# Second expert choice: threshold search by digits and ranks by products, in place of 32 rounds of the eight largest

## The chip, the cores and the metric

The kernel runs on one core of one Trainium2 chip. The metric is the device time of one execution in microseconds (us); before the change it was 1473.17 us, the median of three runs (1472.64 to 1475.16). Work is spread over TensorE (PE in the rows, PEld for its weight loads), VectorE (DVE), ScalarE (ACT), GpSimd (POOL) and the queues of SyncE (SP).

## The reference

Two layers on x of 4 x 1024 tokens of 256 numbers, each a cross attention and a mixture of experts. The change concerns the second mixture, where each expert chooses its tokens. It is this:

```python
k = S // E * CAPACITY            # 1024 // 8 * 2 = 256 tokens for each batch and expert
affinity = softmax(einsum('bsd,ed->bse', x, gate_w), axis=-1)
gating, idx = top_k(transpose(affinity, (0, 2, 1)), k)
x_in = x[bidx, idx]
h = silu(einsum('bekd,eid->beki', x_in, w_gate)) * einsum('bekd,eid->beki', x_in, w_up)
x_e = einsum('beki,edi->bekd', h, w_down)
out = zeros_like(x).at[bidx, idx].add(gating[..., None] * x_e)
```

So there are 32 lists (4 batches x 8 experts) of 256 tokens out of 1024. The order within a list doesn't matter, since the results are added to their tokens; ties at the threshold must go to the lower token number. In front of it stands the second attention: 32 tiles of 128 tokens, 16 heads, 77 keys, then a residual, a second normalisation and the eight gate logits of each token.

## The kernel before

Everything in fp32 precision is done with three products of f16 halves (`mm3`). Each engine has its own program; they meet in semaphores, and each stage's steps are put in an order by hand (`PE_ORDER` and its fellows), run as a software pipeline by `pipeline`: the first and last steps are unrolled, the middle ones run in a loop, unless `straight` asks for all of it unrolled. A `Chain` makes each instruction of a serial computation wait for the one before it.

The second attention (`attn1_*`) runs over 32 tiles t. TensorE makes the transposes, the scores (psS1), the turned probabilities and the outputs; VectorE makes statistics, the row maxima (`largest`, L1571, from psS1 into mx1, then `maxima`, L1580, which scales mx1 in place), the low halves and the residual; ScalarE makes the exponentials and the high halves; GpSimd normalises the probabilities (L1406, L1411). SyncE stores the residual to out_x and the normalised rows to n_rows, 1024 bytes a row. At its end VectorE makes the softmax over the experts: the affinities `aff` (L1616).

The expert choice (`topk_*`) follows. TensorE turns the affinities into 64 rows (each list in two halves) of 512 columns, psA (L1723). VectorE copies them (L1736), and then, 32 times, takes the eight largest of each row (L1739), their places (L1740) and blanks them (L1741), so that each half list has its 256 largest in order. Two such lists are merged: one is turned against the other, and of each pair the larger is one of the 256 largest of the whole (L1742 to L1758). The results are gval (gates) and gidx (token numbers), both with the list in the columns. In this time ScalarE and GpSimd prepare the first expert's weights: ScalarE scales them and makes the high halves (L1706, L1708), GpSimd subtracts these to make the low halves (L1718), two pieces of 3072 columns. SyncE has their loads under way from the last tile of the attention on.

The second expert stage (`ffn1_*`) runs over 16 blocks j of 512 tokens, two for each expert. GpSimd gathers four times 128 rows by gidx (L1785) and at the end adds the results to out_x by the same indices (L1794). TensorE transposes the rows, makes the two up products (psG, psU) for eight pieces f of 128 hidden numbers, then the down product of the block before. ScalarE makes the silu (L1867) and scales the results by gval (L1878); VectorE makes the hidden rows (L1908), their f16 copy (L1911) and their low half (L1913). Both also prepare the next expert's weights piece by piece (L1852, L1891), and the high and low halves of the gathered rows (L1861, L1899).

Of the kernel before, what the change touches and what calls it, by code (L numbers as in the profile page):

```python
# [22 lines left out]
F32 = mybir.dt.float32  # L23
# [122 lines left out]
def program(nc, a, out, tab, n0_rows, x1_rows, n_rows):  # L146
    ctx = ExitStack()
    with ctx:
# [13 lines left out]
        aff = sb("aff", [P, S // P // 2, 2, B, E])  # L162
        gval = sb("gval", [P, 2 * S // E // P, B * E])
# [156 lines left out]
        afff = aff[:].rearrange("p t h b e -> p (t h b e)")  # L320
# [1036 lines left out]
        c_tick = sem("c_tick")  # L1357
# [14 lines left out]
        def apart(e, sem_, value):  # L1372

            wait(e, sem_, value)
            if not isinstance(value, int):
                e.sem_inc(c_tick, 1)

        def attn1_sync(sp):
            def store(t, par):
                sp.wait_ge(c_xn[1], t + 1)  # L1380
                sp.dma_start(out_rows[bass.ds(t * P, P), :], X[:, bass.ds(t, 1), :].rearrange("p t d -> p (t d)"))\
                  .then_inc(c_out[par], 16)
                sp.dma_start(n_rows[bass.ds(t * P, P), :], xn1[1][:, bass.ds(par, 1), :].rearrange("p n d -> p (n d)"))\
                  .then_inc(c_out[par], 16)
            pipeline(sp, T, 1, [(0, store)])
# [34 lines left out]
        def attn1_scalar(act):  # L1420
# [35 lines left out]
            in_order(act, steps, ACT_ORDER, T)  # L1456
# [3 lines left out]
        def attn1_tensor(pe):  # L1460
# [65 lines left out]
            in_order(pe, steps, PE_ORDER, T)  # L1526

        def attn1_vector(dve):
            def stats(n):
                def run(t, par):  # L1530
                    row = X[:, bass.ds(t, 1), :].rearrange("p t d -> p (t d)")
                    if n == 1:
                        apart(dve, c_res, t + 1)
                    dve.bn_stats(st1[n][:], row).then_inc(c_mv[n], 1)
                return run

            def moments(n):
                def run(t, par):
                    apart(dve, c_mv[n], 2 * t + 1)
# [36 lines left out]
            def maxima(half):  # L1576
                def run(t, par):
                    m = mx1[:, half * HP:(half + 1) * HP]
                    dve.wait_ge(c_mx[half], t + 1)
                    dve.tensor_scalar(m, m, -1.0 / (SX * SM), None, ALU.mult).then_inc(c_sub[half], 1)  # L1580
# [20 lines left out]
            in_order(dve, steps, DVE_ORDER, T)  # L1601
# [11 lines left out]
            HT = S // P // 2  # L1613
            for b in range(B):
                tiles = slice(b * 2 * HT, (b + 1) * 2 * HT)
                dve.tensor_tensor(aff[:, :, :, b, :], lex[:, tiles, :].rearrange("p (h t) e -> p t h e", h=2),  # L1616
                                  lsum[:, tiles].rearrange("p (h t) -> p t h", h=2).unsqueeze(3).to_broadcast([P, HT, 2, E]),
# [18 lines left out]
        gx = sb("gx", [P, 2, NT, D], F32, f1)  # L1636
# [8 lines left out]
        HB = 2 * B * E  # L1645
        at_ = sb("at_", [HB, S // 2], F32, f1)
        tv = sb("tv", [HB, CAP], F32, f1)
        ti = sb("ti", [HB, CAP], U32, f1)
        tif = sb("tif", [HB, CAP], F32, f1)
        tvr = sb("tvr", [HB, CAP], F32, f1)  # L1650
        tir = sb("tir", [HB, CAP], F32, f1)
        boff = sb("boff", [P, B * E], F32, f1)
        better = sb("better", [P, SLT, B * E], F32, f1)
        tok = sb("tok", [P, SLT, B * E], F32, f1)
        diff = sb("diff", [P, SLT, B * E], F32, f1)
        f1.close()
        pk = ExitStack()
        psA = ps("psA", [HB, S // 2], F32, pk)
        psV = ps("psV", [P, 4, SLT, HB], F32, pk)
# [18 lines left out]
        d_hid = sem("d_hid")  # L1678
        d_hl = sem("d_hl")
# [6 lines left out]
        k_dve = sem("k_dve")  # L1686
        k_off = sem("k_off")
        k_pe = sem("k_pe")
        ROUNDS = CAP // 8
        KSTEPS = 10 + 3 * ROUNDS  # L1690

# [11 lines left out]

# [6 lines left out]
        def topk_gpsimd(pool):  # L1710
            pool.wait_ge(c_aff, 8)
            pool.iota(boff[:], [[S, B], [0, E]], base=0, channel_multiplier=0,
                      allow_small_or_imprecise_dtypes=True).then_inc(k_off, 1)
# [6 lines left out]
        def topk_tensor(pe):  # L1720
            pe.wait_ge(c_aff, 8)
            for t in range(S // P // 2):
                last = pe.transpose(psA[:, t * P:(t + 1) * P], aff[:, t, :, :, :].rearrange("p h b e -> p (h b e)"), ident[:])  # L1723
            last.then_inc(k_pe, 1)
            pe.wait_ge(k_dve, 3 + 3 * ROUNDS)
            for m, lists in enumerate((tv, tif, tvr, tir)):
                for n in range(SLT):
                    last = pe.transpose(psV[:, m, n, :], lists[:, n * P:(n + 1) * P], ident[0:HB, 0:HB])
            last.then_inc(k_pe, 1)

        def topk_vector(dve):


            ch = Chain(dve, k_dve, 0, KSTEPS)
            dve.wait_ge(k_pe, 1)
            ch(dve.tensor_copy(at_[:], psA[:]))  # L1736
            for r in range(ROUNDS):
                cols = slice(8 * r, 8 * r + 8)
                ch(dve.max(tv[:, cols], at_[:]))  # L1739
                ch(dve.max_index(ti[:, cols], tv[:, cols], at_[:]))  # L1740
                ch(dve.match_replace(at_[:], tv[:, cols], at_[:], -1.0))  # L1741
            ch(dve.tensor_copy(tif[:], ti[:]))  # L1742
            dve.tensor_copy(tvr[:], tv[:, ::-1])
            ch(dve.tensor_copy(tir[:], tif[:, ::-1]))


            first, second = slice(0, B * E), slice(B * E, HB)
            dve.wait_ge(k_pe, 2)
            dve.wait_ge(k_off, 1)
            ch(dve.tensor_copy(gval[:], psV[:, 0, :, first]))  # L1750
            ch(dve.tensor_tensor(better[:], gval[:], psV[:, 2, :, second], ALU.is_ge))
            dve.tensor_tensor(gval[:], gval[:], psV[:, 2, :, second], ALU.max)
            ch(dve.tensor_scalar(tok[:], psV[:, 3, :, second], float(S // 2), None, ALU.add))
            dve.tensor_scalar(gval[:], gval[:], th[:, 3:4], GSC, ALU.mult, ALU.mult)
            ch(dve.tensor_tensor(diff[:], psV[:, 1, :, first], tok[:], ALU.subtract))
            ch(dve.tensor_tensor(diff[:], diff[:], better[:], ALU.mult))
            ch(dve.tensor_tensor(tok[:], tok[:], diff[:], ALU.add))
            ch(dve.tensor_tensor(gidx[:], tok[:], boff[:].unsqueeze(1).to_broadcast([P, SLT, B * E]), ALU.add))  # L1758
            ch.end()
# [14 lines left out]
        def ffn1_gpsimd(pool):  # L1774
# [4 lines left out]
            def gather(j, ph):  # L1779
                wait(pool, d_xt, j - 1)  # L1780
# [15 lines left out]
            pool.wait_ge(k_dve, KSTEPS)  # L1796
            for n in range(2):
                pool.wait_ge(c_out[n], 16 * T)
# [4 lines left out]
        def ffn1_tensor(pe):  # L1803
# [9 lines left out]
            def up(j, ph):  # L1813
# [3 lines left out]
                for f in range(FT1):  # L1817
                    wait(pe, d_hid, 2 * FT1 * j + (2 * f - 3))
# [23 lines left out]
        def ffn1_scalar(act):  # L1842
# [20 lines left out]
            def silu(f):  # L1863
                def run(j, ph):
                    act.wait_ge(d_g, FT1 * j + (f + 1))
                    wait(act, d_hid, 2 * FT1 * j + (2 * f - 3))
# [3 lines left out]
            def results(j, ph):  # L1870
# [3 lines left out]
                for n in range(NT):  # L1874
                    if n % 2 == 0:
                        act.wait_ge(d_y, 2 * j + (n // 2 + 1))
                    col = bass.ds((n % SLT) * (B * E) + ((2 * par + n // SLT) * E) + j // 2, 1)
                    act.activation(yo1[:, par, n, :], psYb[:, n, :], ACT.Copy, scale=gvalf[:, col]).then_inc(d_yo, 1)  # L1878
            gvalf = gval[:].rearrange("p n c -> p (n c)")
# [135 lines left out]
```

## Time and profile before

| | |
|---|---|
| median of 3 runs | 1473.17 us |
| profiled execution | 1480.98 us, its span 1479.2 us |
| PE busy | 1287.0 us (87%) |
| DVE busy | 963.8 us (65%) |
| ACT busy | 643.4 us (43%) |
| POOL busy | 631.9 us (43%) |
| last chain | PE 73%, issue 10%, DVE 7%, ACT 4%, DMA 3% |

The page's slices show three parts: up to about 560 us the first layer and the preparation of the second, from 560 to 857 us the second attention, from 945 us the second experts; in the two slices between, TensorE does nothing. A timeline row reads: start in us, busy us, engine, line, operation, output <- input, count, and in brackets how long the engine was idle before it and what ended that.

### The profile page before, as it was taken

How to read it: one execution, taken by the hardware profiler on the slowest of the kernel's cores; microseconds unless marked ns; L12 is line 12 of the kernel's file. 1: busy time of each engine (PE TensorE's matmuls, PEld its weight loads, DVE VectorE, ACT ScalarE, POOL GpSimd, SP SyncE). 2: the span in 40 equal slices, each digit the busy share in tenths (PEclk: the TensorE clock that was granted, in tenths of full speed). 3: DMA queues.
4: the chain of work that ended last, by engine and by line, in shares of the span. 5: the costliest groups of instructions: out<-in, count | busy, mean ns of one | idle time of the engine just before them, and what ended most of it. 6: DMA issues, size and time to landing. Idle time of an engine off the chain costs nothing.

```text
span 1479.2 us, 30547 instructions
## 1 busy us (share of the span) xinstructions
PE 1287.0 (87%) x9764; PEld 968.2 (65%) x9765; DVE 963.8 (65%) x2109; ACT 643.4 (43%) x2032; POOL 631.9 (43%) x645
## 2 busy tenths in 40 slices
PE   7866598999999987999999910399999999999997
PEld 3755487889999866888888810146665556665555
DVE  3887554655555586888888789486556666555651
ACT  3765122433233366888888730133333333333321
POOL 2287667666666531545445430312333322233213
PEclk8675699999999999999999955699999999999998
DMA  5558234654333340001010120313333322332112
GB/s 164 189 165 192 59 44 59 133 86 64 64 62 65 49 123 1 23 29 36 28 35 28 37 99 0 120 66 75 112 79 83 82 71 71 91 98 37 32 15 29
DMA packets 75079, 107.16 MB, mean 72 GB/s; under 512 B 20278, under 2 KB 66876, under 8 KB 71932
## 3 DMA queue, kind: packets, MB, share of 16 engines
q0 software_dynamic: 29312, 37.31, 15.7%
q1 hardware_dynamic: 44700, 68.62, 14.8%
q8 instruction: 41, 0.67, 0.2%
q10 hardware_dynamic: 992, 0.27, 0.1%
q14 instruction: 34, 0.28, 0.1%
HBM read 69.65 MB, written 36.52 MB: 72 GB/s over the span
## 4 chain that ended last, share of the span: by engine, by line
PE 73%; issue 10%; DVE 7%; ACT 4%; DMA 3%; another core or an unknown queue 1%; POOL 1%; SPq 0%; DVEq 0%; ACTq 0%; POOLq 0%
PE psG L124 6%; PE psU L125 6%; PE psU L124 6%; PE psG L126 6%; PE psU L126 6%; PE psG L125 6%; PE psYb L126 4%; PE psYb L124 4%; PE psYb L125 4%; PE psS L124 2%; PE psS L125 2%; PE psS L126 2%; PE psP L1501 2%; PE psOL L126 2%; PE psOL L124 2%
## 5 line engine op out<-in xcount | busy, mean ns | idle before, releaser
L1794 POOL DMA_INDIRECT out_x<-yo,gidx x64 | 100.9, 1576 | 326.3 <-ACT yo L1878 316.5
L1908 DVE SCALAR_TENSOR_TENSOR hid<-psU,sil 128x512 f32<-128x512 f32 x128 | 88.5, 692 | 186.3 <-ACT sil L1867 185.5
L1867 ACT ACTIVATE sil<-psG 128x512 f32<-128x512 f32 x128 | 76.4, 597 | 214.3 <-PE psU L126 204.8
L981 POOL DMA_INDIRECT x_rows<-yo,tabs x78 | 124.9, 1601 | 100.4 <-ACT yo L1053 79.5
L1448 ACT ACTIVATE pr<-psS,mx 128x77 f32<-128x77 f32 x512 | 158.3, 343 | 5.8 <-DVE mx L1580 3.9
L1080 DVE SCALAR_TENSOR_TENSOR hid<-psU,sil 128x512 f32<-128x512 f32 x78 | 53.8, 690 | 136.9 <-ACT sil L1044 118.5
L125 PE MATMUL psYb<-W1l,hh 128*128 128x256 f16 x512 | 139.6, 273 | 0.0
L126 PE MATMUL psYb<-W1h,hl 128*128 128x256 f16 x512 | 139.6, 273 | 0.0
L124 PE MATMUL psYb<-W1h,hh 128*128 128x256 f16 x512 | 139.6, 273 | 0.0
L1448 ACT ACTIVATION_READ_ACCUMULATOR pr<-psS,mx 128x1 f32 x512 | 115.1, 225 | 0.0
L1044 ACT ACTIVATE sil<-psG 128x512 f32<-128x512 f32 x78 | 46.5, 596 | 145.4 <-PE psU L126 109.3
L1785 POOL DMA_INDIRECT gx<-n_rows,gidx x64 | 67.1, 1048 | 99.2 <-DVE gidx L1758 58.8
L124 PE MATMUL psG<-gxh,W1h 128*128 128x512 f16 x256 | 97.5, 381 | 7.3 <-DVE gxl L1899 5.5
L125 PE MATMUL psG<-gxl,W1h 128*128 128x512 f16 x256 | 97.5, 381 | 0.0
L126 PE MATMUL psG<-gxh,W1l 128*128 128x512 f16 x256 | 97.5, 381 | 0.0
L124 PE MATMUL psU<-gxh,W1h 128*128 128x512 f16 x256 | 97.3, 380 | 0.0
L125 PE MATMUL psU<-gxl,W1h 128*128 128x512 f16 x256 | 97.2, 380 | 0.0
L126 PE MATMUL psU<-gxh,W1l 128*128 128x512 f16 x256 | 97.0, 379 | 0.0
L971 POOL DMA_INDIRECT bx<-n_rows,tabs x78 | 84.0, 1077 | 30.2 <-issue 23.1
L124 PE MATMUL psG<-bxh,Wh 128*128 128x256 f16 x312 | 85.6, 274 | 9.0 <-DVE bxl L1071 5.2
L1913 DVE TENSOR_TENSOR hl<-hid,hh 128x512 f16<-128x512 f32 x128 | 89.0, 695 | 4.4
L124 PE MATMUL psOL<-N,pt 128*128 (+1 forms) x320 | 87.2, 273 | 0.7 <-DVE pt L1563 0.7
(335 smaller groups left out, 3986.7 us busy)
## 6 DMA issues: line engine op xcount, KB each, us to landing
w1s<-in_w SPq DMA_DIRECT2D x16, 1536.0 KB
stage<-in_w SPq DMA_DIRECT2D x8, 1536.0 KB
X<-in_x SPq DMA_DIRECT2D x8, 512.0 KB, 8.9
n_rows<-xc SPq DMA_DIRECT2D x8, 512.0 KB
x_rows<-X SPq DMA_DIRECT2D x8, 512.0 KB
X<-x_rows SPq DMA_DIRECT2D x8, 512.0 KB, 8.2
out_x<-X SPq DMA_DIRECT2D x32, 128.0 KB, 1.7
n_rows<-xn SPq DMA_DIRECT2D x32, 128.0 KB, 1.8
```

Of the source, the lines that this page charges most:

```text
L124: pe.matmul(o, lh, rh, start=first, stop=False)
L125: pe.matmul(o, lh, rl, start=False, stop=False)
L126: return pe.matmul(o, ll, rh, start=False, stop=stop)
L971: pool.indirect_dma_start(bx[:, par, n, :], None, n0_rows[:, :], bass.IndirectOffsetOnAxis(tabs[:, j, n, 0:1], 0)).then_inc(b_in[par], 16)
L981: pool.indirect_dma_start(x1_rows[:, :], bass.IndirectOffsetOnAxis(tabs[:, j, n, 0:1], 0), yo[:, par, n, :], None, compute_op=ALU.add).the ...
L1080: dve.scalar_tensor_tensor(hid[:, half, :, :], psU[half][:, :, :], SH / (SX * SW), sil[:, half, :, :], ALU.mult, ALU.mult).then_inc(b_hid[ ...
L1448: ins = act.activation(pr1[:, par, h * LK:(h + 1) * LK], psS1[:, q, i * LK:(i + 1) * LK], ACT.Exp, bias=mx1[:, h:h + 1], scale=1.0 / (SX * ...
L1785: pool.indirect_dma_start(gx[:, j % 2, n, :], None, n_rows[:, :], bass.IndirectOffsetOnAxis(gidx[:, half, col:col + 1], 0)).then_inc(d_in[ ...
L1794: pool.indirect_dma_start(out_rows[:, :], bass.IndirectOffsetOnAxis(gidx[:, half, col:col + 1], 0), yo1[:, j % 2, n, :], None, compute_op= ...
L1867: act.activation(sil1[:, f % 2, :], psG1[f % 2][:], ACT.Silu, scale=1.0 / (SX * SW)).then_inc(d_sil, 1)
L1908: dve.scalar_tensor_tensor(hid1[:, f % 2, :], psU1[f % 2][:], SH / (SX * SW), sil1[:, f % 2, :], ALU.mult, ALU.mult).then_inc(d_hid, 1)
L1913: dve.tensor_tensor(hl1[:, par, f, :], hid1[:, f % 2, :], hh1[:, par, f, :], ALU.subtract)\
```

## The change

Nothing of the first layer is changed. In the second attention all engines' pipelines are unrolled (`straight`), the counter increments of `apart` are dropped, `largest` writes its eight maxima into unused columns of psS1 and `maxima` reads them there. The affinities are laid out in two halves q, of two batches each. Rows of n_rows get eight numbers more: the token's gates, scaled, written by one transfer from ScalarE's queue; a gather brings them along, and VectorE picks the block's expert out of them.

The choice itself: the threshold of each list, as the bit pattern of the 256th largest value, is found in ten digits of three bits. For each half q the 16 lists are turned into psA with eight copies each, one for each value of a digit. A digit is: count the values that are at least the candidate (one VectorE instruction over 1024 columns, with its sum), compare the count with 256, add up the passed candidates of a list by a product with a 0/1 matrix, and put the digit into the threshold. The two halves take turns. Then the tokens above the threshold and those equal to it are marked, ranked by products with a triangle and with ones, and their slots written out as two one-hot tables (slot div 16, slot mod 16); 16 products for each half place the token numbers, two more put them into the columns of gidx.

In the second expert stage the f16 copy of the hidden rows is made by ScalarE (`hidden_high`) and no longer by VectorE.

```diff
@@ attention
-                dve.tensor_reduce(mx1[:, half * HP:(half + 1) * HP].rearrange("p (q h) -> p q h", q=2),
+                dve.tensor_reduce(psS1[:, 2 * half:2 * half + 2, QK:QK + 4],
...
-                    dve.tensor_scalar(m, m, -1.0 / (SX * SM), None, ALU.mult).then_inc(c_sub[half], 1)
+                    dve.tensor_scalar(m, psS1[:, 2 * half:2 * half + 2, QK:QK + 4], -1.0 / (SX * SM), None, ALU.mult).then_inc(c_sub[half], 1)
...
-            in_order(pe, steps, PE_ORDER, T)
+            in_order(pe, steps, PE_ORDER, T, straight=True)
@@ topk_scalar
+            for q in range(2):
+                act.wait_ge(c_aff, 5 + q)
+                act.activation(affr[:, q], aff[:, q].rearrange("p i b e -> p i (b e)").unsqueeze(2).to_broadcast([P, NI, P // RB, RB]),
+                               ACT.Copy).then_inc(c_le, 1)
+            act.wait_ge(k_set, 15 + DIGITS)
+            for q in range(2):
+                act.activation(affs[:, 2 * q:2 * q + 2], aff[:, q].rearrange("p i b e -> p b i e"),
+                               ACT.Copy, scale=thg[:, 0:1]).then_inc(c_le, 1)
+            act.wait_ge(c_le, 5)
+            act.dma_start(n_rows[:, D:D + E].rearrange("(t p) e -> p t e", p=P), affs[:].rearrange("p b i e -> p (b i) e")).then_inc(c_out[0], 16)
             for j in range(2):
                 act.wait_ge(d_w[j], 16)
@@ topk_tensor
+            for i in range(DIGITS):
+                for q in pairs:
+                    pe.wait_ge(k_dve[q], PASS * i + 2)
+                    pe.matmul(tot[q], same[:].rearrange("p c n -> p (c n)"), passed[:, q:q + 1], start=True, stop=True).then_inc(k_pe, 1)
...
+                pe.matmul(rankp[q], tri1[:], both1, start=True, stop=False)
+                for i in range(1, NI):
+                    pe.matmul(rankp[q][:, :, i * RB:], ones1[:], both1[:, :, 0:(NI - i) * RB], start=False, stop=False)
+                for i in range(NI):
+                    last = pe.matmul(rankp[q][:, 1, :].rearrange("p (i c) -> p i c", c=RB), ones1[:],
+                                     mask2[:, q, 0, i, :].unsqueeze(1).to_broadcast([P, NI, RB]), start=False, stop=i == NI - 1)
@@ topk_vector, after the constants
+            def count(q, i):
+                at = cdig[:, 0:1] if i == 0 else cand[:, q:q + 1]
+                if i == 0:
+                    dve.wait_ge(k_pe, pe_step(0, q))
+                ch[q](dve.tensor_scalar(junk[:], psA[q][:], at.bitcast(F32), None, ALU.is_ge, ALU.add, accum_out=cnt1[:, q:q + 1]))
+                ch[q](dve.tensor_scalar(passed[:, q:q + 1], cnt1[:, q:q + 1], CAP - 0.5, None, ALU.is_ge))
+
+            def digit(q, i):
+                one = slice(q, q + 1)
+                dve.wait_ge(k_pe, pe_step(1 + i, q))
+                ch[q](dve.tensor_scalar(dig[:, one], tot[q], -1.0, float(8 ** (DIGITS - 1 - i)), ALU.add, ALU.mult))
+                if i + 1 < DIGITS:
+                    ch[q](dve.scalar_tensor_tensor(cand[:, one], dig[:, one], thr1[:, one], cdig[:, i + 1:i + 2],
+                                                   ALU.bitwise_or, ALU.bitwise_or))
+                ch[q](dve.tensor_tensor(thr1[:, one], thr1[:, one], dig[:, one], ALU.bitwise_or))
+            for i in range(DIGITS):
+                count(0, i)
+                if i > 0:
+                    digit(1, i - 1)
+                count(1, i)
+                digit(0, i)
+            digit(1, DIGITS - 1)
...
+                ch[q](dve.tensor_tensor(hotA[:, q], sa[:, q].unsqueeze(2).to_broadcast([P, NI * RB, 16]), nums, ALU.is_equal))
+                ch[q](dve.tensor_tensor(hotC[:, q], sc_[:, q].unsqueeze(2).to_broadcast([P, NI * RB, 16]), nums, ALU.is_equal))
+                ch[q](dve.tensor_tensor(hotC[:, q].rearrange("p (i c) n -> p i (c n)", i=NI),
+                                        hotC[:, q].rearrange("p (i c) n -> p i (c n)", i=NI),
+                                        tokv[:].unsqueeze(2).to_broadcast([P, NI, RB * 16]), ALU.mult))
@@ ffn1
-                wait(pool, d_xt, j - 1)
+                wait(pool, d_xl, KD * (j - 1))
...
+            def hidden_high(f):
...
+                    act.activation(hh1[:, par, f, :], hid1[:, f % 2, :], ACT.Copy).then_inc(d_hh, 1)
...
+                dve.tensor_copy(gsc[:, ph, :].unsqueeze(2), gx[:, par, :, bass.ds(D + j // 2, 1)])
```

## Rows read from the trace of the kernel before

**Rows 1.** The page: its span, and the chain that ended last by engine.
```profile
span 1479.2 us, 30547 instructions
...
PE 73%; issue 10%; DVE 7%; ACT 4%; DMA 3%; another core or an unknown queue 1%; POOL 1%; SPq 0%; DVEq 0%; ACTq 0%; POOLq 0%
```

**Rows 2.** Windows: stretch, length, busy by engine, PEclk, DMA share, GB/s.
```profile
640.00:660.00 20.00, 20.00 (x175) 17.31 (x174) 17.89 (x41) 17.36 (x93) 9.95 (x19) 1.00 0.12 39
...
866.00:945.00 79.00, 1.11 (x8) 0.93 (x8) 67.62 (x162) 7.10 (x3) 15.98 (x6) 0.50 0.02 7
...
1000.00:1400.00 400.00, 400.00 (x2519) 247.75 (x2517) 238.73 (x417) 132.01 (x272) 133.91 (x100) 1.00 0.32 76
...
1400.00:1410.00 10.00, 10.00 (x49) 4.48 (x47) 6.99 (x12) 2.39 (x4) 0.00 (x0) 1.00 0.12 16
```

**Rows 3.** Timeline of the expert choice: VectorE's first and last steps, first gather.
```profile
860.07 0.68 DVE L1736 COPY at_<-psA 64x512 f32<-64x512 f32 x1 [1.16 <-PE psA L1723]
860.78 0.69 DVE L1739 MAX8 tv<-at_ 64x8 f32<-64x512 f32 x1
...
933.38 0.67 DVE L1741 MATCH_REPLACE8 at_<-tv,at_ 64x512 f32<-64x512 f32 x1
...
938.00 0.22 DVE L1758 TENSOR_TENSOR gidx<-tok,boff 128x64 int32<-128x64 f32 x1
...
938.51 1.13 POOL L1785 DMA_INDIRECT gx<-n_rows,gidx  x1 [58.76 <-DVE gidx L1758]
```

**Rows 4.** Groups by line and form: busy us, mean ns of one, idle before.
```profile
L1908 DVE SCALAR_TENSOR_TENSOR hid<-psU,sil 128x512 f32<-128x512 f32 x128 | 88.5, 692 | 186.3 <-ACT sil L1867 185.5 <-issue 0.2
...
L1096 DVE SCALAR_TENSOR_TENSOR wq1l<-raw,wq1h 128x2048 f16<-128x2048 f32 x1 | 2.3, 2293 | 3.3 <-ACT wq1h L1064 3.3
...
L1740 DVE MATCH_VALUE_LOAD ti<-tv,at_ 64x8 f32 x32 | 2.7, 83 | 1.1
...
L1593 DVE TENSOR_SCALAR thx<-th 128x1 f32<-128x1 f32 x1 | 0.1, 144 | 0.0
...
L1448 ACT ACTIVATION_READ_ACCUMULATOR pr<-psS,mx 128x1 f32 x512 | 115.1, 225 | 0.0
```

**Rows 5.** Timeline of VectorE at 184 us: small dependent operations.
```profile
184.56 0.17 DVE L636 TENSOR_TENSOR rest<-nblk,taken 128x8 f32<-128x8 f32 x1
184.76 0.17 DVE L637 TENSOR_TENSOR start<-nblk,taken 128x8 f32<-128x8 f32 x1
```

**Rows 6.** Timeline of ScalarE and GpSimd during the expert choice.
```profile
864.92 2.76 ACT L1708 ACTIVATE W1h<-w1s 128x3072 f16<-128x3072 f32 x1
...
867.76 11.98 POOL L1718 TENSOR_TENSOR W1l<-w1s,W1h 128x3072 f16<-128x3072 f32 x2 [8.59 <-ACT W1h L1708]
```

**Rows 7.** Timeline of VectorE beside GpSimd, thrice; one line's duration min/median/max.
```profile
734.92 1.92 POOL L1406 TENSOR_TENSOR pn<-pr,sum 128x1024 f32<-128x1024 f32 x1 [0.20 <-DVE sum L1586]
735.40 1.47 DVE L1580 TENSOR_SCALAR mx<-mx 128x8 f32<-128x8 f32 x1
...
L1580 DVE TENSOR_SCALAR mx<-mx x64: 130/173/1554, 581.4 to 838.5; 128x8 f32<-128x8 f32 x64
...
58.72 1.75 DVE L739 SCALAR_TENSOR_TENSOR Wl<-stage,Wh 128x1536 f16<-128x1536 f32 x1
58.90 2.47 POOL L420 TENSOR_TENSOR rstd<-rstd,mhalf 128x4 f32<-128x4 f32 x1
...
104.69 1.04 POOL L420 TENSOR_TENSOR rstd<-rstd,mhalf 128x4 f32<-128x4 f32 x1
104.82 0.28 DVE L785 TENSOR_TENSOR prod<-rank,pick 128x32 f32<-128x32 f32 x2
```

**Rows 8.** Timeline of TensorE at the lower clock: products of 512 columns.
```profile
949.74 0.63 PE L125 MATMUL psG<-gxl,W1h 128*128 128x512 f16 x1
950.17 0.63 PE L126 MATMUL psG<-gxh,W1l 128*128 128x512 f16 x1
```

**Rows 9.** Timeline of TensorE: the second block's first product.
```profile
978.14 0.39 PE L124 MATMUL psG<-gxh,W1h 128*128 128x512 f16 x1 [3.40 <-DVE gxl L1899]
```

More of the change, by code:

```diff
@@ L1370, in program @@
         POOL_ORDER = [("rstd_in", 0), ("rstd_out", 5), ("normalise_probs", 3)]
[L1372 to L1376, printed above, removed]
         def attn1_sync(sp):
@@ L1532, in run @@
                     if n == 1:
-                        apart(dve, c_res, t + 1)
+                        wait(dve, c_res, t + 1)
                     dve.bn_stats(st1[n][:], row).then_inc(c_mv[n], 1)
@@ L1538, in run @@
                 def run(t, par):
-                    apart(dve, c_mv[n], 2 * t + 1)
+                    wait(dve, c_mv[n], 2 * t + 1)
                     dve.bn_aggr(mv1[n][:, par, :], st1[n][:]).then_inc(c_mv[n], 1)
@@ new lines, in program @@
+        RB = 2 * E
+        DIGITS = 10
+        FAR = float(S)
+        gsc = sb("gsc", [P, 4, NT], F32, f1)
+        affs = sb("affs", [P, B, NI, E], F32, f1)
+        thg = sb("thg", [P, 1], F32, f1)
+        same = sb("same", [P, P // RB, RB], BF16, f1)
+        tri1 = sb("tri1", [P, P], BF16, f1)
+        ones1 = sb("ones1", [P, P], BF16, f1)
+        modf = sb("modf", [P, RB], F32, f1)
+        of_e = sb("of_e", [P, E], F32, f1)
+        ehf = sb("ehf", [P, RB], F32, f1)
+        of_eh = sb("of_eh", [P, RB], F16, f1)
@@ L1656, in program @@
+        own = sb("own", [P, 2, 2, E, 16], F32, f1)
+        toks = sb("toks", [P, 2, 2, 16], F32, f1)
+        turned = sb("turned", [P, 2, 2, 8, 16], F16, f1)
         f1.close()
         pk = ExitStack()
-        psA = ps("psA", [HB, S // 2], F32, pk)
-        psV = ps("psV", [P, 4, SLT, HB], F32, pk)
+        psA = [ps(f"psA{q}", [P, S], F32, pk) for q in range(2)]
+        psK = [ps(f"psK{q}", [P, 512], F32, pk) for q in range(2)]
         pk.close()
@@ L1720, in topk_tensor @@
         def topk_tensor(pe):
[L1721 to L1728, printed above, removed]
@@ L1729, in topk_tensor @@
-            last.then_inc(k_pe, 1)
-        def topk_vector(dve):
[L1734 to L1759, printed above, removed]
@@ new lines, in topk_tensor @@
+            for q in pairs:
+                pe.wait_ge(k_dve[q], D_HOT)
+                for b in range(2):
+                    for i in range(NI):
+                        cols = slice(i * RB + b * E, i * RB + b * E + E)
+                        last = pe.matmul(fillp[q][:, b, :], hotA[:, q, cols, :].rearrange("p e a -> p (e a)"),
+                                         hotC[:, q, cols, :].rearrange("p e c -> p (e c)"), start=i == 0, stop=i == NI - 1)
+                last.then_inc(k_pe, 1)
@@ L1896, in rows_low @@
                 par = ph % 2
+                dve.wait_ge(d_in[par], 16 * NT * (j // 2) + 16 * NT)
+                wait(dve, d_yo, NT * (j - 3) if not isinstance(j, int) or j > 3 else 0)
+                dve.tensor_copy(gsc[:, ph, :].unsqueeze(2), gx[:, par, :, bass.ds(D + j // 2, 1)])
                 for k in range(KD):
```

213 lines of the change are left out of this document (161 added, 52 removed).

## The prediction

> **What bounds the kernel now.** The page gives a span of 1479.2 us, and the chain that ended last is mostly TensorE [rows 1]. That average hides one stage, so I read the windows by stage next. In the second attention (row of 640 to 660 us) and in the second expert stage (1000 to 1400 us) TensorE is busy 20.00 of 20 and 400.00 of 400 us at a granted clock of 1.00; between 866 and 945 us it is busy 1.11 of 79 us, at 0.50, which is the lower of its two levels, 1.2 GHz, while VectorE is busy 67.62 [rows 2]. So two of three stages are bound by TensorE, and the expert choice by one serial chain on VectorE. Its timeline shows what the chain is: copy of the turned affinities at 860.07, then 32 rounds of max, index, replace from 860.78 to 934.05, then the merge of the two half lists to 938.22, and the first gather at 938.51 [rows 3]. A round takes (934.05 - 860.78)/32 = 2.29 us, and nothing else can start the gathers. From the last affinity product (858.9) to the gather are 79.6 us, and every us of it is in the time.
>
> **Reference of the sum.** All durations are of the profiled execution: 1480.98 us, of which 1479.2 are the span. The median of the runs shown is 1473.17, 7.8 lower. I add differences only, and put them on the median.
>
> **The new chain, step by step.** Prices on VectorE: 512 elements with an input in PSUM take 692 ns and 2048 take 2293 [rows 4], so 1.042 ns an element over a fixed part of 0.16; by it 256 take 0.42 and 128 take 0.29. A dependent instruction starts some 0.035 us after the one before. Small two-input operations of 8 elements follow at 0.205 [rows 5]; a one-element operation is 144 ns long against their 168 [rows 4], so I take 0.19 for the mean of the one-element ones.
> (a) Constants on VectorE, 19 dependent instructions: five of 128 elements at 0.32 and 14 small ones at 0.19, 4.3 us, from 858.9 to 863.15. They stand ahead of the first count, in the place of a wait of 1.16 us. GpSimd's six are issued earlier, behind the last attention tile. Beside them ScalarE copies the affinities (two of 1024 elements, about 1.0 each by its 2.76 for 3072 [rows 6]) and TensorE turns them: four transposes lay in the 1.16 us that VectorE waited for them [rows 3], so eight take some 2.1; the first pair's are there at 861.9, the second's at 863.9 for a count at 864.6. Covered; bare it would cost up to 1 us.
> (b) Ten digits for two interleaved halves. A count reads 1024 elements of PSUM: 1.23 + 0.035. The sum that it leaves behind is unpriced in this trace: nothing (0) at one end, a separate read like ScalarE's 0.225 at the other [rows 4]; nearest on VectorE is the 83 ns of the value load in front of a search [rows 4], so 0.08. Then one compare (0.19) and three digit operations (0.57). That is 2.10 us, 20 times 42.0; the last digit has two operations fewer (-0.4), and the last TensorE round trip is bare (+0.3): 41.9, to 905.05. The other round trips (about 0.45) lie behind the other half's count. What is late next if that cover goes is the digit itself, 20 times 0.45 at worst.
> (c) Two broadcast copies, a turn, four masks of 128 elements: 6 times 0.32 and 0.2 of waiting, 2.1, to 907.15.
> (d) Ranks: 16 products of 2176 columns in all for each half. Cold, 512 columns follow at 0.43 [rows 8], so 1.83 and 0.4 of start and drain; VectorE idles 1.55 for the first half, the second is covered.
> (e) Slots and the two one-hot tables: 0.46, three of 0.32, three of 2048 elements at 2.33: 8.4 for each half, 16.8, to 925.5. This is the second large term.
> (f) 16 fill products of 2048 columns, 2.15; then three of 256 elements (1.4); list products and indices 0.85; 0.3 to the gather. To 930.2.
> Nothing in the way, the gather starts 8.3 us before 938.5. Removed: everything in [rows 3].
>
> **What runs beside it.** The low halves of the first weights, two GpSimd subtractions of 3072 elements that took 11.98 us back to back, waited for ScalarE's high halves [rows 6]. ScalarE now first waits for the constants (863.15), makes two small copies and issues a transfer, about 864.0, and needs two passes of 2.76 until the first high half: GpSimd runs from 869.6 to 881.6, inside (b). Before, VectorE ran searches with a single SBUF input there, untouched. Now two of the five digit operations (the candidate, the threshold) read both inputs from SBUF. What the trace shows of this pair: VectorE's 8-element scaling in SBUF started at 735.40 and ended at 736.87, with GpSimd's multiply, 734.92 to 736.84 [rows 7]; its median is 173 ns, its maximum 1554. And with VectorE first, on two SBUF inputs (58.72 to 60.47), GpSimd's small power took 2.47 us instead of 1.04 [rows 7]. So they exclude each other for whole instructions. Against it: two products with both inputs in SBUF went through undisturbed (0.28 for both) while that same power ran, 104.69 to 105.73 [rows 7]; but it has four elements and can have read them long before, whereas the subtraction streams 3072. I take it as blocked: of 12.0 us, VectorE uses on average 0.65 until it first meets such an operation, one more gets through between the two subtractions, and 11.3 are lost. The gather moves to 941.5, 3.0 later than before. Bounds: 0 and 12.0.
> The Trainium skill, page "SBUF — State Buffer", section "Who interferes with whom", says that a VectorE instruction with two SBUF inputs contends with a GpSimd instruction that reads SBUF, and that whoever comes first has the shared pair for the whole instruction. By that rule the stall is the 11.3; without it the sum is the 8.3 gained. The trace agrees in two of three rows, and no row has exactly this pair.
> The page "VectorE: DVE Perf Modes", section "Two Vector instructions with no wait between them", says that an operation that writes out its accumulator is two instructions, the main one and a read; no row here shows it on VectorE.
>
> **The transfer of the gates.** 4096 pieces of 32 B behind ScalarE at 864; it has until the gather, 66 us. The DMA was at 0.02 of its engines in that stretch [rows 2], so nothing. The rows gathered grow from 1024 to 1056 B: 0.1 us for the first four.
>
> **Attention.** The unrolled code, the dropped counter increments and the row maxima that go through PSUM save VectorE at least the waits of [rows 7]. TensorE is at 20.00 of 20 there, so this is worth nothing. The last blocks of the second expert stage run unrolled already, and TensorE is at 10.00 of 10 us there (1400 to 1410 [rows 2]), so longer code is no stall either. Bounds: -1 (the last tile) and +2 (code that comes late after all).
>
> **Second expert stage.** The f16 copy of the hidden rows goes from VectorE to ScalarE. TensorE stays full, so it is free except where the pipeline fills: TensorE waited 3.40 us at 978.14 for the second block's low rows [rows 9]. ScalarE's last copy now stands in front of the high rows, about 0.5 later; VectorE drops its own and gains a small gate copy in front of the low rows; together +0.2, between -0.4 and +0.9. A gather now waits for the low rows of the block before last instead of their transposes, but it runs two blocks ahead of its use.
>
> **Sum.** +3.0 +0.1 +0.2 = +3.3 us: 1480.98 becomes 1484.3, and the median 1473.17 + 3.3 = 1476.5. A measurement here tells some 0.2% (2.9 us) from no change.
>
> **Rivals.**
> 1. The port lets the one-element operations through (as it did at 104.82), or the subtractions slip past the digits. Then the gather is at 930.2: 1473.17 - 8.3 + 0.3 = 1465.2, faster by 0.5%. For: the undisturbed row; against: the scaling of 8 elements, as small, that waited out its partner.
> 2. The count costs more: a read of the sum at 0.25 instead of 0.08 is 3.4 us in 20 counts, 0.1 more on each of the six table operations 0.6; with the lock 1476.5 + 4.0 = 1480.5. Without the lock it alone would make the change slower from 0.4 us more a count (8.0 / 20).
> 3. Attention gets shorter after all, or the clock of TensorE rises in the expert choice and with it (d), (f) and the first products: -2 to -3 with the lock, 1474.
>
> **How the numbers follow.** Forecast 0.62, own range 1473.5 to 1480 (the sum's read between 0 and 0.2, fill and rank products 1 us either way); rival 1 0.26; rival 2 0.07; rival 3 0.05. The range has to reach rival 1 (1465.2 less 1.7 for its own spread): 1463.5 to 1480.5, leaving out about 0.13. Slower by over 0.2% (over 1476.1): 0.33 of the forecast's 0.62, and rival 2, 0.40. Within: 0.27 and 0.03, 0.30. Faster: 0.26, and 0.04 of the others, 0.30.
>
> **What would show it.** The first gather at 941.5 (lock) or 930.2; in VectorE's timeline two small digit operations of 5 to 6 us each that end with GpSimd's subtractions; counts 1.26 to 1.35 apart from the next; table operations of 2.29; the first gather followed by the same start of the expert stage. The prediction is wrong if the digit operations stay at 0.2 beside the subtractions, if a count is not near 1.3, or if the attention's end moves by over 1 us.

## The result

The changed kernel takes 1476.49 us (median of 20 runs) beside 1473.03 of the kernel before (20 runs): ratio 1.0024, 95% interval 1.0014 to 1.0033, so 3.5 us slower. A second comparison, on a chip where every kernel ran some 1% longer, gave 1491.09 beside 1487.81: 1.0014, 0.9995 to 1.0034, which alone would not tell the two apart. The forecast was 1476.5 for the first.

The page of the changed kernel:

```profile
span 1475.3 us, 29168 instructions
## 1 busy us (share of the span) xinstructions
PE 1306.2 (89%) x9858; PEld 986.1 (67%) x9859; DVE 860.0 (58%) x1989; ACT 709.9 (48%) x2164; POOL 629.2 (43%) x650
```

Its windows, as [rows 2] (the choice's window moved to where the choice now lies; columns: stretch, length, busy by engine, PEclk, DMA share, GB/s):

```profile
640.00:660.00 20.00, 20.00 (x176) 17.36 (x174) 13.91 (x37) 15.86 (x84) 11.01 (x18) 1.00 0.09 29
852.00:931.00 79.00, 13.43 (x97) 10.28 (x95) 72.19 (x153) 11.63 (x6) 11.96 (x2) 0.52 0.06 14
1000.00:1400.00 400.00, 400.00 (x2501) 245.91 (x2500) 186.19 (x328) 182.58 (x369) 132.89 (x100) 1.00 0.33 76
```

VectorE's busy time fell by 103.8 us, and the kernel is not faster. The windows say why: TensorE is at 20.00 of 20 and 400.00 of 400 before and after, so what VectorE gave up in these two stages was time that lay hidden behind TensorE. Only the choice is VectorE's own, and there it is still busy 72.19 of 79 us. An operation that is held up counts as busy, so this figure contains the 10.9 us of stall that are shown below.

The page shows a second oddity: the span of this execution is 3.9 us shorter than that of before [rows 1], though the medians say longer. So I cut the spans at three events: TensorE's first transpose of the attention, the end of the affinities on VectorE, and the first gather. In us, of ten traces (the experiments are explained below):

| trace | span | first layer | attention | expert choice | gather to end |
|---|---|---|---|---|---|
| before | 1479.2 | 575.9 | 283.0 | 79.6 | 540.7 |
| changed | 1475.3 | 564.6 | 284.0 | 83.1 | 543.6 |
| e3, the kernel before again | 1472.1 | 565.3 | 284.7 | 79.6 | 542.6 |
| changed again | 1486.0 | 577.6 | 284.0 | 83.1 | 541.3 |
| e1 | 1461.3 | 563.8 | 283.2 | 72.3 | 542.0 |
| e2 | 1475.7 | 568.5 | 284.1 | 80.5 | 542.6 |
| e4 | 1474.8 | 571.4 | 283.0 | 79.6 | 540.9 |
| e5 | 1484.3 | 581.2 | 282.8 | 79.6 | 540.7 |
| e6 | 1478.5 | 580.1 | 284.2 | 72.4 | 541.9 |
| e7 | 1471.5 | 575.5 | 282.8 | 71.3 | 541.9 |

The first layer, whose code nobody touched, moves by over 10 us between two executions of one kernel (575.9 and 565.3). Part of this can be the chip: on the chip of e1 to e4 it took 563.8 to 571.4 us, on that of e5 to e7 and of the second trace of the changed kernel 575.5 to 581.2. The means are 11.4 us apart, of the 12.9 us by which the kernel before is longer there (1487.81 beside 1474.87). For the first two traces the chip isn't on record, and the profiled execution of the kernel before, 1480.98 us, lies above all of its 20 runs (1467.26 to 1475.31). The choice repeats to 0.1 us, on either chip. It is 3.5 us longer, and that fits the 3.5 of the medians. A span of one trace could not have shown this; a stage of one trace does.

Inside the choice, VectorE's timeline of the changed kernel, from the end of the affinities (columns: start, us, engine, line, operation, and in brackets the idle time before it and what ended it):

```profile
848.14 0.49 DVE L1607 TENSOR_TENSOR aff<-lex,lsum 128x128 f32<-128x128 f32 x2
848.55 0.36 DVE L1817 TENSOR_REDUCE modf<-ident 128x16 f32<-128x128 f32 x1
...
852.94 1.28 DVE L1835 TENSOR_SCALAR_CACHE_REDUCE junk<-psA,cdig 128x1024 bf16<-128x1024 f32 x1
...
860.49 5.34 DVE L1843 SCALAR_TENSOR_TENSOR cand<-dig,thr,cdig 128x1 int32<-128x1 int32 x1
865.87 5.92 DVE L1845 TENSOR_TENSOR thr<-thr,dig 128x1 int32<-128x1 int32 x1
871.82 1.28 DVE L1835 TENSOR_SCALAR_CACHE_REDUCE junk<-psA,cand 128x1024 bf16<-128x1024 f32 x1
873.03 0.08 DVE L1835 DVE_READ_ACCUMULATOR junk<-psA,cand 128x1 f32 x1
873.15 0.16 DVE L1836 TENSOR_SCALAR passed<-cnt 128x1 bf16<-128x1 f32 x1
873.34 0.16 DVE L1841 TENSOR_SCALAR dig<-psK 128x1 int32<-128x1 f32 x1
873.53 0.22 DVE L1843 SCALAR_TENSOR_TENSOR cand<-dig,thr,cdig 128x1 int32<-128x1 int32 x1
873.79 0.16 DVE L1845 TENSOR_TENSOR thr<-thr,dig 128x1 int32<-128x1 int32 x1
873.98 1.28 DVE L1835 TENSOR_SCALAR_CACHE_REDUCE junk<-psA,cand 128x1024 bf16<-128x1024 f32 x1
...
906.51 0.49 DVE L1854 COPY thrb<-thr 128x128 f32<-128x128 f32 x2
...
909.96 0.42 DVE L1863 SCALAR_TENSOR_TENSOR slot<-psK,mask 128x256 f32<-128x256 f32 x1 [1.52 <-PE psK L1794]
910.41 0.29 DVE L1865 SCALAR_TENSOR_TENSOR sloti<-slot 128x128 int32<-128x128 f32 x1
910.74 0.23 DVE L1866 TENSOR_SCALAR sa<-sloti 128x128 int32<-128x128 int32 x1
...
911.26 2.29 DVE L1869 TENSOR_TENSOR hotA<-sa,iota 128x2048 f16<-128x2048 int32 x1
...
926.52 0.42 DVE L1876 TENSOR_TENSOR own<-psK,of_e 128x256 f32<-128x256 f32 x1
...
930.08 0.84 DVE L1885 TENSOR_SCALAR gidx<-psK 128x16 int32<-128x16 f32 x4
```

And of GpSimd, as [rows 3] and [rows 6]:

```profile
859.81 11.96 POOL L1769 TENSOR_TENSOR W1l<-w1s,W1h 128x3072 f16<-128x3072 f32 x2 [14.54 <-ACT W1h L1752]
...
931.73 1.12 POOL L1914 DMA_INDIRECT gx<-n_rows,gidx  x1 [59.96 <-issue]
```

Two operations on one element a partition last 5.34 and 5.92 us. One digit later the same two last 0.22 and 0.16. The first ends at 865.83 and the second at 871.79; the subtraction pair runs from 859.81 to 871.77. That is the stall: (5.34 - 0.22) + (5.92 - 0.16) = 10.9 us, three times the 3.5 by which the choice grew.

### The profile page after: what moved, and what is told of

It reads as the page before. It is cut to its first block, busy times and chain, and to the rows that moved or that the text cites. A ratio compares the mean times of both kernels' runs of the same rounds, so it can differ in the third digit from the quotient of the medians.

```text
span 1475.3 us, 29168 instructions
## 1 busy us (share of the span) xinstructions
PE 1306.2 (89%) x9858; PEld 986.1 (67%) x9859; DVE 860.0 (58%) x1989; ACT 709.9 (48%) x2164; POOL 629.2 (43%) x650
## 4 chain that ended last, share of the span: by engine, by line
PE 72%; DVE 10%; DMA 6%; issue 4%; POOL 4%; ACT 2%; SPq 1%; POOLq 0%; ACTq 0%; DVEq 0%
PE psG L124 5%; PE psU L124 5%; PE psU L125 5%; PE psG L125 5%; PE psU L126 5%; PE psG L126 5%; PE psYb L124 4%; PE psYb L126 4%; PE psYb L125 4%; PE psS L124 3%; PE psS L125 2%; PE psS L126 2%; PE psP L1493 2%; PE psOL L126 2%; PE psOL L125 2%
## 5 line engine op out<-in xcount | busy, mean ns | idle before, releaser
L980 POOL DMA_INDIRECT x_rows<-yo,tabs x78 | 124.6, 1597 | 94.6 <-ACT yo L1052 71.3
L1440 ACT ACTIVATION_READ_ACCUMULATOR pr<-psS,mx 128x1 f32 x512 | 118.2, 231 | 0.0
L124 PE MATMUL psOL<-N,pt 128*128 128x256 f16 x320 | 87.2, 273 | 0.6 <-DVE pt L1555 0.6
```

The costliest lines, as they stand in the source:

```text
L124: pe.matmul(o, lh, rh, start=first, stop=False)
L980: pool.indirect_dma_start(x1_rows[:, :], bass.IndirectOffsetOnAxis(tabs[:, j, n, 0:1], 0), yo[:, par, n, :], None, compute_op=ALU.add).the ...
L1440: ins = act.activation(pr1[:, par, h * LK:(h + 1) * LK], psS1[:, q, i * LK:(i + 1) * LK], ACT.Exp, bias=mx1[:, h:h + 1], scale=1.0 / (SX * ...
```

## The experiments

Four questions: does the stall come from operands in SBUF that VectorE and GpSimd read at the same time, and would the new choice be faster without it (e1, e2); how much does a second trace of the same code vary (e3, and the changed kernel again); are the attention and the hidden copy worth nothing (e4, e5); what is left to gain (e6, e7). Ratios are against the kernel before, run on the same chip; e1 to e4 shared one chip, the other four another.

### e1: the digit in PSUM

```
+        digp = [p[:, 8:9].bitcast(I32) for p in psK]
...
-                ch[q](dve.tensor_scalar(dig[:, one], tot[q], -1.0, float(8 ** (DIGITS - 1 - i)), ALU.add, ALU.mult))
+                ch[q](dve.tensor_scalar(digp[q], tot[q], -1.0, float(8 ** (DIGITS - 1 - i)), ALU.add, ALU.mult))
...
-                ch[q](dve.tensor_tensor(thr1[:, one], thr1[:, one], dig[:, one], ALU.bitwise_or))
+                ch[q](dve.tensor_tensor(thr1[:, one], thr1[:, one], digp[q], ALU.bitwise_or))
```

The candidate (L1844 in this kernel) takes its digit from PSUM in the same way. No operation is added or dropped; the two that stalled now read one operand less from SBUF.

> The changed kernel, but the digit is written to a free column of the totals' PSUM bank instead of to SBUF, so that the candidate and the threshold operation read only one tensor from SBUF each. Nothing else is moved. Port theory: the two operations of 5.34 and 5.92 us beside GpSimd's subtractions fall back to about 0.2 each, the stretch from the end of the affinities to the first gather falls from 83.1 to 72.2 us, and the time by 10.9 us against the changed kernel, to about 7.5 below the kernel before (ratio 0.995). Rival (the operations were long for another reason, such as the one before them in the queue or integers in SBUF while GpSimd runs): the stretch stays at 83.

Measured: 1466.74 us beside 1474.87, ratio 0.9955 (0.9939 to 0.9972). VectorE of this kernel:

```profile
858.87 0.22 DVE L1844 SCALAR_TENSOR_TENSOR cand<-psK,thr,cdig 128x1 int32<-128x1 int32 x1
859.12 0.15 DVE L1846 TENSOR_TENSOR thr<-thr,psK 128x1 int32<-128x1 int32 x1
...
860.64 0.16 DVE L1837 TENSOR_SCALAR passed<-cnt 128x1 bf16<-128x1 f32 x1
...
861.03 0.22 DVE L1844 SCALAR_TENSOR_TENSOR cand<-psK,thr,cdig 128x1 int32<-128x1 int32 x1
861.29 0.15 DVE L1846 TENSOR_TENSOR thr<-thr,psK 128x1 int32<-128x1 int32 x1
```

and GpSimd of the same kernel:

```profile
858.18 6.02 POOL L1770 TENSOR_TENSOR W1l<-w1s,W1h 128x3072 f16<-128x3072 f32 x1 [15.23 <-ACT W1h L1753]
```

The same operations run at full speed in the middle of the subtraction. The choice is 72.3 us, 10.8 shorter than with the digit in SBUF, and 7.3 shorter than before. The theory had said 72.2 us, and 7.5 us less than the kernel before; the medians differ by 8.1. So the stall needs the digit in SBUF, and it alone turns a gain of 0.5% into a loss of 0.2%. Integers in SBUF as such are not the reason: the threshold still lies there. That the two engines exclude each other is shown by this; what in the chip they share, no run shows.

### e2: the subtraction after the digits

```
             for j in range(2):
...
+                pool.wait_ge(k_dve[1], D_THR)
                 pool.tensor_tensor(W1l[:, 0, cols], w1s[:, j, :], W1h[:, 0, cols], ALU.subtract).then_inc(d_firstl, 1)
```

> The changed kernel, with GpSimd's two subtractions held until all ten digits are done, so that they run beside the masks, slots and one-hot tables. Port theory: the digits lose their 10.9 us of stall, and the tables of 2048 elements, which read two tensors from SBUF, get it instead: a table or slot operation is 5 to 6 us long twice, and the first gather comes within 2 us of where it came in the changed kernel. Rival (only the one-element operations suffer): the tables stay at 2.29 us and the gather comes 10 us earlier.

Measured: 1474.68 us, ratio 1.0004 (0.9985 to 1.0023), choice 80.5. VectorE and GpSimd of this kernel:

```profile
903.01 0.42 DVE L1864 SCALAR_TENSOR_TENSOR slot<-psK,mask 128x256 f32<-128x256 f32 x1 [1.52 <-PE psK L1795]
903.47 2.91 DVE L1866 SCALAR_TENSOR_TENSOR sloti<-slot 128x128 int32<-128x128 f32 x1
906.41 5.89 DVE L1867 TENSOR_SCALAR sa<-sloti 128x128 int32<-128x128 int32 x1
912.34 0.23 DVE L1868 TENSOR_SCALAR sc_<-sloti 128x128 int32<-128x128 int32 x1
```

```profile
900.23 12.00 POOL L1770 TENSOR_TENSOR W1l<-w1s,W1h 128x3072 f16<-128x3072 f32 x2 [51.03 <-DVE thrb L1855]
```

The digits are undisturbed, and the stall has gone to the next operations of the kind: 2.62 + 5.66 = 8.3 us. It is 2.6 shorter than in the changed kernel because the first 3.2 us of the subtraction fell on masks and slots with one operand in PSUM and on VectorE's idle 1.52. The expectation was right in its theory and missed in two details: the slot operations took the whole stall and every table stayed at 2.29, and the gather came 2.6 us earlier, where at most 2 had been expected. Moving the heavy instruction moved the stall; taking an operand out of SBUF ended it.

### e3: the kernel before once more, and the changed kernel once more

> The kernel before, unchanged, beside itself: ratio 1.000. It is here for its stages. In the two profiles at hand the first layer, which the change doesn't touch, took 574.1 us to the attention's first aggregate in the kernel before and 562.7 in the changed one. If that is chance from run to run, this profile falls anywhere between; if the changed kernel's code really shortens it, this one is near 574 again.

Measured: 1473.85 us, ratio 1.0007 (0.9991 to 1.0023). Its trace has the first layer at 565.3 us where the first trace of the same code had 575.9, and a choice of 79.6 both times. So the shorter first layer of the changed kernel's first trace is no work of its code.

> The changed kernel once more, for its stages beside those of its first trace. Theory (the 3.5 us longer expert choice is the whole of the difference and the rest is chance of the execution): choice 83.1 us, attention 283.0 to 284.7, first attention transpose anywhere in 563.8 to 575.9, the stretch behind the gather 540.7 to 543.6 and shorter where the granted clock does not fall at the second block; ratio 1.002 to 1.003. Rival (the change itself lengthens the second expert stage by some 2 us, since its first trace shows 543.6 against 540.7 and 542.6 of the kernel before): 543.6 again, with the second block's first products at 0.61 ns per 512 columns in us again.

Measured: ratio 1.0014 (0.9995 to 1.0034), choice 83.1, gather to end 541.3; the two operations that stall took 5.34 and 5.91 us. The first layer, 577.6 us, lay above the range that was expected, and the ratio below its own. The 543.6 of the first trace was chance, and the place of it can be named. TensorE's first product of the second block, and the windows behind it, in the changed kernel:

```profile
971.46 0.61 PE L124 MATMUL psG<-gxh,W1h 128*128 128x512 f16 x1 [3.48 <-DVE gxl L2041]
```

```profile
971.46:976.46 5.00, 5.00 (x12) 1.79 (x13) 0.00 (x0) 0.00 (x0) 3.78 (x4) 0.50 0.87 355
976.46:981.46 5.00, 5.00 (x23) 2.23 (x22) 2.41 (x5) 2.53 (x5) 0.00 (x0) 0.95 0.11 32
```

and in the second trace of the changed kernel:

```profile
984.97 0.39 PE L124 MATMUL psG<-gxh,W1h 128*128 128x512 f16 x1 [3.48 <-DVE gxl L2041]
```

```profile
984.97:989.97 5.00, 5.00 (x24) 2.29 (x25) 1.16 (x2) 1.01 (x2) 3.78 (x4) 1.00 0.87 353
```

After the same idle 3.48 us the granted clock was 0.50 once, the lower level of 1.2 GHz, and 1.00 the other time. Nothing in the code differs, and why the clock does is open. From that product to the end took 503.8 us in the first case and 501.0 in the second; 5 us at 0.50 and 5 at 0.95 are 2.75 us of work not done, which is the difference. The kernel before does the same: 1.00 in its first trace (501.1 us to the end), and 0.66 over the first 5 us in e3 (502.8, where 5 x 0.34 = 1.7 is expected).

### e4: the attention's edits alone

In the kernel before, the attention's pipelines were unrolled and the row maxima sent through PSUM, as the change does:

```
-                    dve.tensor_scalar(m, m, -1.0 / (SX * SM), None, ALU.mult).then_inc(c_sub[half], 1)
+                    dve.tensor_scalar(m, psS1[:, 2 * half:2 * half + 2, QK:QK + 4], -1.0 / (SX * SM), None, ALU.mult).then_inc(c_sub[half], 1)
...
-            in_order(dve, steps, DVE_ORDER, T)
+            in_order(dve, steps, DVE_ORDER, T, straight=True)
```

> The kernel before with the attention's edits alone: all its pipelines unrolled, the row maxima through PSUM (the counter increments stay). The maxima's scaling falls from a mean of 777 ns to about 170. TensorE is full in this stage, so I expect a ratio of 1.000 and the stretch from the first transposes to the affinities within 1 us of 283.0. Rival (unrolled code costs fetches): 1 to 2 us longer, as the changed kernel's 284.0 hints. A second rival is a gain of some us before this stage, since the profile of the changed kernel reached it 11 us earlier.

Measured: ratio 0.9999 (0.9983 to 1.0015), attention 283.0 us. Neither rival holds: the attention is no longer than before, and the ratio shows no gain ahead of it. The group of the scaling in this kernel (busy us, mean ns of one, idle before):

```profile
L1580 DVE TENSOR_SCALAR mx<-psS 128x8 f32<-128x8 f32 x64 | 10.3, 161 | 1.1
```

Its maximum before was 1554 ns [rows 7]; in the changed kernel min, median and max are 133, 165 and 168 ns:

```profile
L1572 DVE TENSOR_SCALAR mx<-psS x64: 133/165/168, 570.3 to 828.4; 128x8 f32<-128x8 f32 x64
```

So the same cure, at the attention, removes the long ones among 64 operations, and it is worth nothing: TensorE was the bound there.

### e5: the hidden copy on ScalarE alone

```
             def hidden(f):
...
-                    dve.tensor_copy(hh1[:, par, f, :], hid1[:, f % 2, :]).then_inc(d_hid, 1)
...
+            def hidden_high(f):
...
+                    act.activation(hh1[:, par, f, :], hid1[:, f % 2, :], ACT.Copy).then_inc(d_hh, 1)
```

> The kernel before with one part of the change alone: the f16 copy of each hidden tile made once, by ScalarE, instead of by both engines. My theory (this edit is worth nothing on average, +0.2 us in the sum, bounds -0.4 to +0.9): ratio 1.000, the stretch from first gather to the end within the 540.7 to 543.6 us that the traces so far show, the wait before the second block's first product 3.4 to 3.6 us. Rival (the edit delays every block's second weight products): the stretch is over 544.5 us and the ratio at least 1.002.

Measured: ratio 0.9999 (0.9981 to 1.0018), gather to end 540.7 as before, wait before the second block 3.42 us where before had 3.40 [rows 9]. This edit is worth nothing that can be told from zero.

### e6: the next block's rows ahead of the last hidden tile

On e1, in ScalarE's and in VectorE's order of work:

```
-            work.append((2, hidden_high(FT1 - 1)))
-            pipeline(act, NB1, DD, work + [(1, rows_high), (3, results)], unroll=4)
+            work += [(1, rows_high), (2, hidden_high(FT1 - 1))]
+            pipeline(act, NB1, DD, work + [(3, results)], unroll=4)
```

> The changed kernel with the digit in PSUM, and in the second expert stage ScalarE's and VectorE's split of the next block's rows put ahead of the last hidden tile's copy and subtraction. Theory (the second block waits for VectorE's gxl, which stands behind the last hl): the wait before the second block's first product falls from 3.48 to about 2.6 us, 1 us shorter than the kernel with the digit in PSUM alone (ratio about 0.9948 against before, where that one had 0.9955), and the granted clock after that wait may stay high. Rival (the row split only changes places with the hidden tile, for which the down product of every block then waits): the wait before the second block shrinks but one of 0.5 to 1 us appears before each block's last down products, and the stretch from first gather to the end grows by 1 us or more.

Measured: 1479.83 us beside 1487.81, ratio 0.9940 (0.9917 to 0.9963). The second block's first product:

```profile
975.91 0.61 PE L124 MATMUL psG<-gxh,W1h 128*128 128x512 f16 x1 [2.88 <-DVE gxl L2042]
```

The wait fell from 3.48 to 2.88 us, 0.6 where 0.9 was expected. The gather to the end took 541.9 us beside 542.0 of e1, both with a lowered clock behind the wait (0.71 and 0.73 over 5 us): of the 0.6 only 0.1 is left. Of the rest, 0.3 is an earlier wait for `hid`, 1.68 us here and 1.35 in e1, which lies anywhere from 1.0 to 2.3 in these traces. No new wait appeared in the steady part, so the rival does not hold. The clock did not stay up either. Whether e6 beats e1 can't be told from two intervals that overlap this far.

### e7: six constants made early

On e6, six of VectorE's constants issued ahead of its wait for the router's products:

```
+            first_constants(dve)
             dve.wait_ge(c_lg, T)
...
+        def first_constants(dve):
+            dve.wait_ge(c_av[2], T)
...
+            st_ = Chain(dve, c_one, 0, 6)
...
+            st_(dve.tensor_reduce(modf[:], eye.rearrange("p (c n) -> p n c", n=RB), AX.X, ALU.add))
```

> As the run before it, and six of the constants that VectorE makes for the counting (modf, same, of_e, ehf, of_eh, of_a8) stand ahead of its wait for the router's products, at the end of the attention stage, instead of behind the affinities. Theory (these 1.4 us stood alone on the path, VectorE being idle while it waits for the router): end of affinities to first count falls from 4.3 to about 2.9 us, end of affinities to first gather from 72.3 to about 70.9, the ratio 0.001 below the run before it. Rival (the constants wait for ScalarE's transposed copy or GpSimd's own constants and tables, which end the wait anyway): the first count starts when TensorE's transposes of the affinities are done, and less than 0.5 us is gained.

Measured: 1479.35 us beside 1487.81, ratio 0.9937 (0.9911 to 0.9962), choice 71.3. VectorE of this kernel:

```profile
853.17 0.36 DVE L1820 TENSOR_REDUCE modf<-ident 128x16 f32<-128x128 f32 x1
...
854.69 0.38 DVE L1825 TENSOR_REDUCE of_a<-ident 128x8 f32<-128x128 f32 x1
855.62 0.42 DVE L1598 TENSOR_REDUCE lmx<-psOL 128x32 f32<-128x256 f32 x1 [0.55 <-PE psOL L1483]
...
860.50 0.15 DVE L1837 TENSOR_SCALAR thg<-th 128x1 f32<-128x1 f32 x1
861.44 1.28 DVE L1845 TENSOR_SCALAR_CACHE_REDUCE junk<-psA,cdig 128x1024 bf16<-128x1024 f32 x1 [0.78 <-PE psA L1780]
```

The six filled the idle time before the router's products. e6's trace is no measure for it, since TensorE ran its last products of the attention there at a granted clock of 1.00 and VectorE waited 1.62 us; here the clock was 0.50, as good as in e1 (0.52), where the same wait without the constants is 2.29:

```profile
844.29 0.42 DVE L1597 TENSOR_REDUCE lmx<-psOL 128x32 f32<-128x256 f32 x1 [2.29 <-PE psOL L1483]
```

From 2.29 to 0.55 are 1.7 us filled. But only 1.0 of the 1.9 us that the six occupy came out at the gather (72.4 in e6, 71.3 here): the first count now waits 0.78 us for TensorE's transposes of the affinities, the wait that the constants had covered. The theory had the larger part, the rival named the wait that kept the rest. The first count fell from 4.3 to 3.1 us behind the affinities, where the theory had 2.9 and the rival 3.8 or more. This version has the lowest ratio of all, though the intervals of e6 and e1 overlap its own; it is 0.8% under the changed kernel on the same chip (1479.35 beside 1491.09, and its longest run, 1482.71, is under the other's shortest, 1483.44) and 0.6% under the kernel before.

## Why the prediction was right

By its own steps, from the end of the affinities (858.9 in the forecast, 848.6 in the changed kernel's trace):

| step | forecast us | measured us | from |
|---|---|---|---|
| (a) constants to first count | 4.3 | 4.3 | 848.6 to 852.94 |
| (b) ten digits without the stall | 41.9 | 42.7 | 852.94 to 906.51, less 10.9 |
| the stall | 11.3 | 10.9 | 5.12 + 5.76 |
| (c) copies, turn, masks | 2.1 | 1.9 | 906.51 to 908.44 |
| (d) wait for ranks | 1.55 | 1.52 | bracket at 909.96 |
| (e) slots and tables | 16.8 | 16.5 | 909.96 to 926.5 |
| (f) fill, lists, start of the gather | 4.7 | 5.2 | 926.5 to 931.73 |
| sum | 82.6 | 83.1 | |

- (b) A count with its digit takes 2.16 us (871.82 to 873.98) where the forecast had 2.10. The count itself takes 1.21 until its read starts, 0.05 less than put. The read is 0.08 long, as its nearest row [rows 4] had it, but 0.12 with the start of the next, which the forecast left out; and the candidate, with its three inputs, takes 0.26 to the next start instead of 0.19. That is +0.06 net, twenty times +1.2. The end of the last digit takes off 0.4 of it: the last TensorE round trip, put at +0.3, was covered (no idle time stands in front of its digit), and the two candidates that are left out save more than put. So (b) is +0.8, the largest miss of a step.
- The stall. Its size, the two operations and their ends were forecast; e1 shows the cause by removal. The rule of the Trainium skill, page "SBUF — State Buffer", section "Who interferes with whom", is the mechanism that the forecast took; the sum made it 11.3 us, and the trace agrees with the rule, at 10.9. The row against it, the products of 32 elements beside the power of four elements, did not carry over to this pair. Why it went through is not tested; that the power has only four elements to read, and the subtraction 3072, is the forecast's reason and fits.
- (f) The index operation ends at 930.92 and the gather starts at 931.73, 0.8 later; the forecast had taken the 0.3 of before [rows 3]. This is the miss of (f), it is 0.8 in e1, e2 and the second trace of the changed kernel too, and why no run here tells.
- Attention, forecast 0: 284.0 twice, where the kernel before shows 283.0 and 284.7, and e4 283.0: right. Hidden copy and second block, +0.2: the wait grew by 0.08 (3.48 beside 3.40), and e5 by 0.02: right, and less than I had put. Gates, 0, and longer rows, +0.1: the transfer is issued at 853.66 and lands 5.7 us later, the DMA engines are at 0.00 from 864 us to the gather at 931.73, and nothing waits for it: right. The 0.1 itself can't be told, as the waits for `hid` behind the gathers vary by more.
- Rival 1, that the one-element operations slip through, is refuted in the changed kernel and realised in e1, which came out 8.1 us below the kernel before where the rival had been put 8.0 below. Rival 2, a dearer read of the sum or dearer tables, is refuted by 0.08 and by tables of 2.29. Rival 3 is refuted by the clock of 0.52 in the choice and the attention's unchanged length.

The sum said +3.3 and the choice alone gives +3.5. That the median was met to 0.01 us is chance: the sum's terms were off by +0.8, +0.5, -0.4, -0.3 and -0.2, which cancel in part, and the median of 3 runs from which it started lay 0.14 from that of 20. Of the profiled executions the forecast was off by 7 us (1484.3 beside 1477.06): it fell on an execution with a first layer 11.3 us shorter.

## What to carry to other kernels

Before small VectorE operations on a serial path are put beside a long GpSimd instruction, look where their operands lie: one operand moved to PSUM was worth 10.8 us here, and delaying the GpSimd instruction moved the stall and took 2.6 us off it. Count the busy time that a change removes only in stages whose bound is that engine; 103.8 us less of VectorE brought nothing where TensorE was full. And compare traces by stage, on one chip: two traces of the same code differed by 10 us in a part that no edit touched, and two chips by as much, while the stage in question repeated to 0.1.

## What the runs showed of the hardware

- A VectorE operation of one element with its inputs in SBUF waits until the GpSimd subtraction under way has ended (5.34 and 5.92 us beside two instructions of some 6.0, 5.34 and 5.91 in the second trace), and VectorE got exactly one turn between two such instructions that follow back to back, here and in e2.
- An operation with a single SBUF input was held as well: the shift `sa`, int32 in SBUF to int32 in SBUF, took 5.89 us in e2 beside the second subtraction and 0.23 undisturbed, while in the choice of before the single-input searches had gone on untouched, and in e1 the one-element `passed`, f32 in SBUF to bf16 in SBUF, took 0.16 in the middle of the subtraction. In the same 128 elements the two-input `sloti` takes 0.29. The Trainium skill, page "VectorE: DVE Perf Modes", section "Mode 2×_2P — use both read ports for one tensor", has a faster mode for one-source operations from SBUF to SBUF that takes both read ports; the 0.23 beside 0.29 would fit that, and no run here separates it.
- An operation that leaves its sum behind is two rows on VectorE: 1.28 us for 1024 elements of PSUM, and a read of 0.08. The same page of the Trainium skill, section "Two Vector instructions with no wait between them", says that it is two instructions; the trace agrees and gives the price of the second.
- TensorE's granted clock after an idle time of 3.40 to 3.48 us in front of the second block was 1.00 over the next 5 us in four traces and 0.50 to 0.73 in the other four, of the same or nearly the same code, worth up to 2.8 us; an idle time of 2.88 us in e6 and e7 did not prevent it either (0.71 and 0.66 over the first 5 us).
